# Two graph layers on one core: the second layer's preparation moved into the attention block, its roots on GpSimd, and fewer unused products at the start

## The chip, the core and the metric

The kernel runs on one core of a Trainium2 chip. TensorE (PE, with its weight loads PEld), VectorE (DVE), ScalarE (ACT) and GpSimd (POOL) each work through their own queue in order; SyncE (SP) issues the transfers. They meet at semaphores. The metric is the device time of one execution in microseconds, lower is better.

## What is computed

Two layers on x (4096 x 128 fp32) with one 0/1 adjacency matrix adj (4096 x 4096 int32). Layernorm has no scale or shift.

```python
h = relu(layernorm(x))
q, k, v = (h @ W.T + b for each)                       # 128 x 128 weights
scores = where(adj > 0, q @ k.T / sqrt(128), -9e15)
x = x + elu(softmax(scores, axis=-1) @ v)
h = relu(layernorm(x))
hw = h @ W
s1, s2 = hw @ a[:128], hw @ a[128:]
e = where(adj > 0, leaky_relu(s1[:, None] + s2[None, :], 0.01), -9e15)
x = x + hw + softmax(e, axis=1) @ h
```

## The kernel before, in words

x lies in SBUF as 32 tiles of 128 rows (T = 32), in 8 chunks of 4 tiles (NC = 8). A strip is one tile of query rows against all 4096 keys. The program has four blocks; at a block's end every engine waits for all.

**First stage** (`norm_and_project` with `x_in`, line 68). `constants_in` (line 390) starts with WARM = 36 products that nobody reads. Then, chunk by chunk: VectorE takes moments (`moments_of`), ScalarE the root (`roots`), VectorE the inverse, GpSimd normalises (line 104), TensorE transposes (`to_hT`, line 220) and makes the q, k and v products; ScalarE and VectorE copy out high and low parts. VectorE copies the turned weights (`copy_turned`, line 381) after its third chunk of moments, and TensorE's second transposes stand behind them. At the end come the extras: the turned weight of layer two, its product with a, and the bias row (`extras`, `copy_extras`). GpSimd makes the mask of strip 0 (`first_strip`).

**Attention block.** Each strip s has a period. TensorE (`period`, from line 863) makes strip s + 1's and s + 2's scores in four parts of 1024 columns (`make_scores`, 3 products per 512 columns, lines 810 to 812), turns strip s's weights (`turn`, `turn_high`, lines 821 and 837) and multiplies by v (`times_v`, lines 856, 857). VectorE adds the mask and finds the maximum (`add_mask`, line 726) and makes low parts (`low_part`, line 745, SBUF to SBUF; `turned_low`, line 738); ScalarE makes exponentials (line 647) and copies (lines 654, 661, 669). GpSimd's period is `add_elu(s - 2)`, `make_mask(s + 2)` (line 309), `add_halves(s - 1)` (lines 608, 610), `make_bytes(s + 3)` (line 304). SP loads adj, stores the mask bytes and turns the low parts by transposing transfers (`turn_low`). ScalarE's `elu_exp(s - 1)` closes its period, behind GpSimd's `add_halves(s - 1)`, and strip s + 1's first copies are queued behind it. The last strips have less to do: no mask for GpSimd after strip 29's period, no scores for TensorE after strip 30's.

**Second preparation** (`norm_and_project` again, without `x_in`). It begins when the attention block has ended. VectorE makes all 32 variances and the inverse roots, ScalarE the root, and then for each chunk: VectorE normalises (line 181), TensorE transposes, and the three jobs follow: `s_product` (s1 and s2 per row, 8 small products) with ScalarE's exponentials and VectorE's `weigh` (line 989, two instructions of 128 x 512); `s1_product` (s1 as a row on all partitions) with a copy and the signs; `hw_product` with VectorE's `hw_add` (line 1029). The signs compare each key's s2 with the queries' s1: for the first group of four strips `first_signs` and `first_sign` make 32 tiles of 128 x 512 bytes (ScalarE line 922 three of four, VectorE line 927 one). GpSimd's `split_words` (line 1018) makes the bf16 low parts of the weighed keys. SP loads the mask bytes of the first two groups by eight transposing transfers (`first_masks`). At the end `find_top` finds the largest s2 and a flag that chooses between the fast and a general path (always the fast one here), with three small products in between (`spread_top`), and cuts the first strip's mask.

**Second layer** (the `fast` functions). For each group g of 4 strips and strip b, VectorE's `cut(g, par, b)` combines mask bits and signs (`scale_mask`, `cut_lower`, `cut_upper`, lines 938, 942, 947), TensorE multiplies 64 pairs of tiles (line 1381), ScalarE copies the sums out (`copy_sums`, line 1316), VectorE forms the result and SP stores it. ScalarE's `body(g)` copies four strips' s1 (`s1_block`), and makes the signs of group g + 1, 11, 11 and 10 of them ahead of the sums of strips 0, 1 and 2. `cut(g + 1, ., 0)` waits for all 32 (`signs_ready`).

## Time and profile before

| | us |
|---|---|
| three runs | 771.25, 771.36 (median), 771.85 |
| the profiled execution | 769.68 |
| its span, first to last instruction | 767.9 |
| TensorE busy | 731.9 (95%) |
| VectorE, ScalarE, GpSimd busy | 564.3, 549.4, 432.9 |

"Busy" adds up an engine's instructions; a busy TensorE is one with a product under way, whatever its clock. The page cuts the span into 40 slices of 19.2 us and gives each engine's share in tenths, and beside it the TensorE clock that was granted. A timeline row has start, duration, engine, line, operation, output<-input and, in brackets, the engine's idle time before it and who released it. Where an engine's next instruction starts before the end of the one in front, rows overlap: the time from start to start is what the queue costs.

### The profile page before, as it was taken

To read this page: it belongs to the slowest core of one execution; us is meant where nothing else is said; L and a number is where in the kernel's file an instruction comes from. 1 tells how busy PE (TensorE), PEld (TensorE's weight loads), DVE (VectorE), ACT (ScalarE), POOL (GpSimd) and SP (SyncE) were. 2 spreads that over 40 slices of the span, in tenths; PEclk is the share of its full clock that TensorE was granted. 3 is DMA by queue.
4 is the path that set the end of the run, shared out by engine and by line. 5 is a ranking of instruction groups with operands and counts; after the bars stand their busy time and mean duration, and the time that the engine had idled before them with its cause. 6 is when DMAs were issued, how large, how long until landed. Compare 5 with 4: busy or idle time off the path is not lost. (4 is left out here: it accounts for less than half of the span.)

```text
span 767.9 us, 18394 instructions
## 1 busy us (share of the span) xinstructions
PE 731.9 (95%) x6301; PEld 616.8 (80%) x6301; DVE 564.3 (73%) x1199; ACT 549.4 (72%) x1063; POOL 432.9 (56%) x349
## 2 busy tenths in 40 slices
PE   8979999999999999999999997785999999999996
PEld 7658888888888888888888886554888888888885
DVE  5968787878878787877878784698477576577572
ACT  3846868787786878777786867685877977987910
POOL 5688799999999999999999963351000000000000
PEclk9989999999999999999999999697999999999999
DMA  6189998998979898887989742820253534433100
GB/s 234 60 286 252 243 269 240 280 252 253 258 251 262 235 279 238 276 257 245 258 252 269 220 97 56 168 53 0 63 91 65 94 76 80 92 74 80 38 10 13
DMA packets 189324, 130.88 MB, mean 170 GB/s; under 512 B 170336, under 2 KB 176992, under 8 KB 181088
## 3 DMA queue, kind: packets, MB, share of 16 engines
q1 hardware_dynamic: 188544, 130.05, 62.1%
q8 instruction: 25, 0.41, 0.2%
q10 hardware_dynamic: 576, 0.26, 0.1%
q14 instruction: 19, 0.16, 0.1%
q0 software_dynamic: 160, 0.00, 0.0%
HBM read 69.47 MB, written 18.87 MB: 115 GB/s over the span
## 5 line engine op out<-in xcount | busy, mean ns | idle before, releaser
L1381 PE MATMUL ps_x<-v,big 128*128 128x258 bf16 x2048 | 232.2, 275 | 2.3 <-issue 2.3
L1381 PEld LDWEIGHTS ps_x<-v,big 128*128 128x128 fp8e4 x2048 | 199.0, 98 | 32.6 <-issue 2.4
L726 DVE CUSTOM_DVE_ANT_0 scores<-ps_s,mask_neg 128x1024 f32<-128x1024 f32 x128 | 155.8, 1217 | 17.3 <-POOL mask_neg L309 17.0
L647 ACT ACTIVATE scores<-scores,neg_max 128x1024 f32<-128x1024 f32 x128 | 146.1, 1143 | 17.8 <-DVE neg_max L732 17.8
L745 DVE TENSOR_TENSOR low<-scores 128x1024 bf16<-128x1024 f32 x96 | 136.8, 1425 | 28.6 <-ACT scores L647 28.6
L309 POOL TENSOR_SCALAR mask_neg<-mask_bytes 128x2048 bf16<-128x2048 uint8 x64 | 153.3, 2396 | 5.4 <-POOL mask_bytes L304 0.4
L304 POOL TENSOR_SCALAR mask_bytes<-adj_sb 128x2048 uint8<-128x2048 int32 x64 | 148.2, 2332 | 3.4 <-POOLq L80 1.7
L661 ACT ACTIVATE hiT<-ps_t 128x512 bf16<-128x512 bf16 (+1 forms) x128 | 103.0, 805 | 53.4 <-PE ps_t L837 50.7
L856 PE MATMUL ps_acc<-v_parts,hiT 128*128 128x256 bf16 x768 | 140.4, 273 | 0.7 <-DMA lowT<-low 0.4
L922 ACT ACTIVATE big<-s_block,s_col 128x512 fp8e4<-128x512 f32 x224 | 139.4, 717 | 0.0
L857 PE MATMUL ps_acc<-v_parts,lowT 128*128 128x128 bf16 x768 | 133.6, 219 | 0.0
L810 PE MATMUL ps_s<-k_hi,q_strip 128*128 128x512 f32 x256 | 112.6, 440 | 3.6 <-DVE row_max L726 2.5
L812 PE MATMUL ps_s<-k_hi,q_strip 128*128 128x512 f32 x256 | 102.3, 400 | 0.0
L811 PE MATMUL ps_s<-k_lo,q_strip 128*128 128x512 f32 x256 | 101.0, 394 | 0.0
L856 PEld LDWEIGHTS ps_acc<-v_parts,hiT 128*128 128x128 bf16 x768 | 75.1, 98 | 8.6 <-issue 0.8
L857 PEld LDWEIGHTS ps_acc<-v_parts,lowT 128*128 128x128 bf16 x768 | 75.1, 98 | 0.7
L1316 ACT ACTIVATE sums<-ps_x,ac 128x258 f32<-128x258 f32 x64 | 26.6, 467 | 64.5 <-PE ps_x L1381 64.5
L738 DVE TENSOR_TENSOR pT_low<-ps_t,pT_high 128x512 bf16<-128x512 f32 x64 | 44.0, 687 | 31.1 <-ACT pT_high L654 31.1
L837 PEld LDWEIGHTS ps_t<-ident_half,scores 128*128 128x128 bf16 x768 | 44.9, 98 | 25.5 <-issue 25.1
L837 PE MATMUL ps_t<-ident_half,scores 128*128 128x128 bf16 x768 | 64.9, 221 | 0.0
L654 ACT ACTIVATE pT_high<-ps_t 128x512 bf16<-128x512 f32 x64 | 37.6, 590 | 34.8 <-PE ps_t L821 33.9
L810 PEld LDWEIGHTS ps_s<-k_hi,q_strip 128*128 128x128 f32 x256 | 48.9, 191 | 11.9 <-DVE row_max L726 3.3
(144 smaller groups left out, 1010.3 us busy)
## 6 DMA issues: line engine op xcount, KB each, us to landing
adj_sb<-in_adj SPq DMA_DIRECT2D x64, 1024.0 KB, 5.3
mask_bytes_dram<-mask_bytes SPq DMA_DIRECT2D x32, 512.0 KB, 2.9
x_sb<-in_x SPq DMA_DIRECT2D x8, 256.0 KB, 7.8
out<-res SPq DMA_DIRECT2D x32, 64.0 KB, 1.6
lowT<-low SPq DMA_TRANSPOSE x96, 4.7
big<-mask_bytes_dram SPq DMA_TRANSPOSE x32, 4.6
raw_w<-in_L_gnn_Wq ACTq DMA_DIRECT2D x1, 64.0 KB, 3.2
raw_w<-in_L_gnn_Wk ACTq DMA_DIRECT2D x1, 64.0 KB, 3.8
```

The costliest lines, as they stand in the source:

```text
L304: return nc.gpsimd.tensor_scalar(mask_bytes[par][:, half(h)], adj_sb[h][:], 1.0, 0.0, ALU.min, ALU.max)
L309: return nc.gpsimd.tensor_scalar(out, src, -NEG, NEG, ALU.mult, ALU.add)
L647: nc.scalar.activation(sc, sc, ACT.Exp, bias=neg_max[:, bn:bn + 1], accum_out=row_sum[:, bn, k:k + 1]).then_inc(exp_done, 1)
L661: nc.scalar.activation(hiT[k][:, half_of], ps_t[(2 + u) % 3][:].bitcast(BF16)[:, half_of], ACT.Copy).then_inc(hiT_ready, 1)
L726: nc.vector.tensor_tensor_reduce(out=scores[bn % 2][:, part(k)], in0=ps_s[k % 2][:], in1=mask[bn % 2][:, part(k)], scale=1.0, scalar=LOWES ...
L745: nc.vector.tensor_tensor(low[k][:], p, high_half(p), ALU.subtract).then_inc(low_done, 1)
L810: nc.tensor.matmul(o, high, k_hi[:, col], start=True, stop=False)
L837: last = nc.tensor.transpose(out[:, D * t:D * t + D], high[:, D * t:D * t + D], ident_half[:])
L856: nc.tensor.matmul(ps_a[:], high, v_parts[:, t, :, :], start=(i == 0 and n == 0), stop=False)
L857: last = nc.tensor.matmul(ps_a[:, 0, :], rest, v_parts[:, t, 0, :], start=False, stop=(i == NC - 1 and n == 3))
L922: return nc.scalar.activation(by_key_tile(lower[par], t), src.rearrange("p (s i) -> p s i", s=4), ACT.Sign, bias=s_col[:, t, 1:2], saturat ...
L1381: last = nc.tensor.matmul(ps_x[b % 2][k][:], by_key_tile(m, t)[:, b], v1[k][:, t, :].bitcast(BF16), start=(t == 0), stop=(t == T - 1))
```

## The change

The separate second preparation is taken away; its steps stand in the attention block's queues, around and behind the periods of the last strips.

- SBUF is laid out anew so that the preparation's tensors lie over tensors of the attention that are dead by then: h_sb over adj_sb, hT2 over scores[0], s1_row over the masks, v1 over q, the mask and sign tiles over k, scores[1] and v_parts. Four PSUM banks (`spare`) serve the first stage, the attention and the hw products in turn.
- Inverse roots are found without ScalarE's table, by a first guess from the bits (VectorE, `MAGIC`) and three Newton steps: for tiles 0 to 23 on GpSimd in the period of strip 29 (8 + 12 small operations on 24 columns, with VectorE's guess between them), for tiles 24 to 31 on VectorE at the end. GpSimd normalises chunks 0 to 2 in that period and 3 to 5 in the next; VectorE chunks 6 and 7. Both ScalarE table changes to Sqrt and back go.
- TensorE turns chunks 0, 1 and 2 and makes the first s products and the first 512 columns of s1 inside strip 31's period; ScalarE copies these out there.
- The last strip's attention output is finished by VectorE instead of ScalarE and GpSimd.
- Of s1 only the first 512 columns are made as a row by a product. The rest is stored from the column form to DRAM, one 4-byte element at a time (`store_s1`), and loaded back to all partitions in the second layer's block; ScalarE waits for it before group 1's and group 2's signs.
- Group 0's signs are made for strips 0 and 1 in the preparation, all 32 tiles by ScalarE, half as wide; those for strips 2 and 3 at the start of the second layer's block, 16 tiles on VectorE and 16 on ScalarE. In group 0 ScalarE makes group 1's signs 16 ahead of the sums of strip 1 and 16 ahead of those of strip 2, instead of 11, 11 and 10. Four of the eight hw additions move there too.
- Chunks 3 to 6 have one of two weighings on ScalarE.
- In the first stage WARM is 14, and the extras run inside chunks 3 to 5. At the start of the attention VectorE's `add_mask(1, 1, 1)` stands in front of `low_part(0, 0, 0)`.

```diff
-WARM = 36
+WARM = 14
...
+                def extras(pe, c):
+                    if c == 3:
+                        pe.wait_ge(weight_in, 16)
+                        nc.tensor.transpose(pw[:, 3 * D:4 * D], raw[3][:], ident[:]).then_inc(turn_done, 1)
+                    if c == 4:
+                        pe.wait_ge(turn_read, 4)
+                        pe.wait_ge(vectors_in, 16 * len(vectors))
+                        nc.tensor.matmul(pw[:, 0:2], turned[3][:], a_cols[:], start=True, stop=True)
+                        nc.tensor.matmul(pw[:, D:2 * D], ones[0:1, :], bv_row[:], start=True, stop=True).then_inc(extras_done, 1)
...
+                    def store_s1(cs, i):
+                        sp.wait_ge(s_out, cs.stop)
+                        for c in range(cs.start, cs.stop):
+                            sp.dma_start(s1_dram[c].rearrange("t p -> p t"), s_col[:, 4 * c:4 * c + 4, 0],
+                                         allow_slow_non_contiguous=True).then_inc(s1_stored[i], 16)
...
+                    sp.wait_ge(s_ready, 4 * T)
+                    for b in range(4):
+                        load_mask(sp, 0, b, 0)
+                    store_s1(S1_CHUNKS[0], 0)
+                    sp.wait_ge(t_done, TURNS * T)
+                    sp.wait_ge(low_done, 3 * T)
+                    for b in range(4):
+                        load_mask(sp, 1, b, 1)
+                    store_s1(S1_CHUNKS[1], 1)
...
+                    def inverse_root(cs):
+                        steps = Steps(pool, pool_tail)
+                        bn, moments, rstd = stats["bn"][:, cs], stats["moments"][:, cs], stats["rstd"][:, cs]
+                        mean_e, mean_o, m2_e, m2_o = (bn[:, :, i] for i in (1, 4, 2, 5))
+                        mean, var, apart, work = moments[:, :, 0], moments[:, :, 1], stats["root"][:, cs], newton[:, cs]
+                        pool.wait_ge(bn_done, cs.stop)
+                        steps.mark(nc.gpsimd.tensor_tensor(apart, mean_e, mean_o, ALU.subtract))
+                        steps.mark(nc.gpsimd.tensor_tensor(mean, mean_e, mean_o, ALU.add))
+                        steps.do(nc.gpsimd.tensor_tensor(var, m2_e, m2_o, ALU.add))
+                        steps.mark(nc.gpsimd.tensor_tensor(work, apart, apart, ALU.mult))
+                        steps.mark(nc.gpsimd.tensor_scalar(minus_mean[:, cs], mean, -0.5, 0.0, ALU.mult, ALU.add))
+                        steps.do(nc.gpsimd.tensor_scalar(var, var, 1.0 / D, EPS, ALU.mult, ALU.add))
+                        steps.do(nc.gpsimd.tensor_scalar(work, work, 0.25, 0.0, ALU.mult, ALU.add))
+                        steps.mark(nc.gpsimd.tensor_tensor(var, var, work, ALU.add))
+                        steps.wait()
+                        pool.sem_inc(var_made, 1)
+                        pool.wait_ge(seed_made, 1)
+                        for _ in range(3):
+                            steps.do(nc.gpsimd.tensor_tensor(work, rstd, rstd, ALU.mult))
+                            steps.do(nc.gpsimd.tensor_tensor(work, work, var, ALU.mult))
+                            steps.do(nc.gpsimd.tensor_scalar(work, work, -0.5, 1.5, ALU.mult, ALU.add))
+                            steps.do(nc.gpsimd.tensor_tensor(rstd, rstd, work, ALU.mult))
...
+                        if last_ones and s == T - 3:
+                            inverse_root(FIRST)
+                            pool.wait_ge(bytes_ready, 2 * T)
+                            for n in range(3):
+                                normalise(n)
+                        if last_ones and s == T - 2:
+                            for n in range(3, 6):
+                                normalise(n)
...
+                        if not ahead:
+                            act.wait_ge(low_done, 3 * T - 3)
+                            hT_out(0)
...
                             elu_exp(s - 1)
+                    def hT_out(c):
+                        act.wait_ge(x_turned, c + 1)
+                        nc.scalar.activation(hT2[:, 512 * c:512 * c + 512], turned_x[c % 2], ACT.Relu,
+                                             accum_out=hT_sum[:, c:c + 1]).then_inc(hT_ready, 1)
...
+                    def early_signs(c):
+                        act.wait_ge(s_out, c + 1)
+                        act.wait_ge(s1_out, 1)
+                        for t in range(4 * c, 4 * c + 4):
+                            last = sign_bytes(0, s1_row, t, EARLY)
+                        if c == NC - 1:
+                            last.then_inc(signs_ready, 1)
+                    def weigh(c):
+                        act.wait_ge(s_out, c + 1)
+                        for t in range(4 * c, 4 * c + 4):
+                            last = nc.scalar.activation(v1[0][:, t, 0:D], h_sb[:, t, :], ACT.Relu, scale=v1[0][:, t, D:D + 1])
+                        last.then_inc(weighed_by_scalar, 1)
                     all_periods(act, period)
-                    acc_copy(T - 1, 3)
-                    elu_exp(T - 1)
-                    use_table(1, ACT.Sqrt)
+                    s_out_of(0)
+                    act.wait_ge(s1_made, 1)
+                    nc.scalar.activation(s1_row[:, 0:512], ps_s3[1], ACT.Copy).then_inc(s1_out, 1)
+                    hT_out(2)
+                    act.wait_ge(last_att, 1)
+                    act.wait_ge(epi_done, T - 1)
+                    nc.scalar.activation(att_neg[:], att[:], ACT.Relu, scale=-1.0).then_inc(att_cut, 1)
+                    nc.scalar.activation(att_pos[:], att[:], ACT.Relu)
+                    act.wait_ge(att_cut, T)
+                    nc.scalar.activation(att_exp[:], att_neg[:], ACT.Exp, scale=-1.0).then_inc(last_parts, 1)
+                    s_out_of(1)
+                    hT_out(3)
+                    early_signs(0)
+                    for c in range(2, NC):
+                        s_out_of(c)
+                        if c + 2 < NC:
+                            hT_out(c + 2)
+                        if c in BY_SCALAR:
+                            weigh(c)
+                        early_signs(c - 1)
+                    early_signs(NC - 1)
...
+                    def last_attention():
+                        b = (T - 1) % 2
+                        inv = inv_by_parity[:, b:b + 1]
+                        dve.wait_ge(pv_done, 8 * T)
+                        dve.wait_ge(inv_ready, T)
+                        dve.wait_ge(halves_added, T - 1)
+                        dve.wait_ge(att_ready, T - 1)
+                        nc.vector.scalar_tensor_tensor(out=acc_sb[:, 0, :], in0=ps_a[:, 1, :], scalar=inv, in1=bv_rep[:],
+                                                       op0=ALU.mult, op1=ALU.add).then_inc(last_half, 1)
+                        dve.wait_ge(att_exp_ready, T - 1)
+                        dve.wait_ge(last_half, 1)
+                        nc.vector.scalar_tensor_tensor(out=att[:], in0=ps_a[:, 0, :], scalar=inv, in1=acc_sb[:, 0, :],
+                                                       op0=ALU.mult, op1=ALU.add).then_inc(last_att, 1)
...
                     add_mask(1, 1, 0)
+                    add_mask(1, 1, 1)
                     low_part(0, 0, 0)
-                    add_mask(1, 1, 1)
...
+                        if isinstance(c, int) and s == T - 3:
+                            dve.wait_ge(var_made, 1)
+                            first_guess(FIRST)
+                            tail.wait()
+                            nc.vector.sem_inc(seed_made, 1)
...
                     inverse_sum(T - 1, 3)
-                    for s in range(T - 3, T):
-                        dve.wait_ge(epi_done, s + 1)
-                        moments_of(s)
+                    dve.wait_ge(epi_done, T - 2)
+                    moments_of(T - 3)
+                    dve.wait_ge(epi_done, T - 1)
+                    moments_of(T - 2)
+                    aggregate(slice(LAST.start, T - 1))
+                    weigh(0)
+                    last_attention()
+                    weigh(1)
+                    last_elu()
+                    aggregate(slice(T - 1, T))
+                    add_eps(LAST)
+                    inverse_root(LAST)
+                    normalise(NC - 2)
+                    normalise(NC - 1)
+                    for c in range(2, NC - 1):
+                        weigh(c)
+                        if c >= 3:
+                            add_hw(c - 3)
+                    dve.wait_ge(s_out, NC)
+                    tail.mark(nc.vector.tensor_reduce(out=hT_total[:], in_=hT_sum[:], axis=AX.X, op=ALU.add))
+                    nc.vector.tensor_reduce(out=top[:, 0:1], in_=s_col[:, :, 1], axis=AX.X, op=ALU.max)
+                    tail.do(nc.vector.tensor_reduce(out=top[:, 1:2], in_=s_col[:, :, 0:2], axis=AX.XY, op=ALU.max,
+                                                    apply_absolute_value=True))
+                    nc.vector.tensor_scalar(hT_diag[:], ident[:], hT_total[:], None, ALU.mult).then_inc(top_ready, 1)
+                    weigh(NC - 1)
+                    dve.wait_ge(words_in[0], 64)
+                    scale_mask(0, 0).then_inc(scaled_ready, 1)
+                    dve.wait_ge(top_t, 1)
+                    nc.vector.tensor_copy(h_sum[:], ps_s2[:, D:2 * D])
+                    tail.do(nc.vector.tensor_reduce(out=top_turned[:], in_=ps_s2[0:2, 0:D], axis=AX.X, op=ALU.max))
+                    nc.vector.tensor_scalar(top_diag[:], ident[0:2, 0:2], top_turned[:], None, ALU.mult).then_inc(top_d, 1)
+                    dve.wait_ge(scaled_ready, 1)
+                    dve.wait_ge(signs_ready, 1)
+                    cut_lower(0, 0).then_inc(lower_ready, 1)
+                    dve.wait_ge(top_b, 1)
+                    tail.do(nc.vector.tensor_copy(top[:], ps_s2[:, 0:2]))
...
+                        if not ahead:
+                            pe.wait_ge(masked, 4 * T)
+                            turn_h(0)
...
+                        if not ahead:
+                            turn_h(1)
...
+                        if not ahead:
+                            s_products(0)
+                            nc.tensor.matmul(ps_s3[1], wa_rep[:], hT2[:, 0:512], start=True, stop=True).then_inc(s1_made, 1)
...
+                        if not ahead:
+                            turn_h(2)
...
+                    def turn_h(c):
+                        if c < NC - 2:
+                            pe.wait_ge(h_ready, c + 1)
+                        else:
+                            pe.wait_ge(h_by_vector, c - NC + 3)
...
+                        for i, cs in enumerate(S1_CHUNKS):
+                            sp.wait_ge(s1_stored[i], 16 * (cs.stop - cs.start))
+                            row = s1_dram[cs.start:cs.stop].rearrange("c t p -> (c t p)")
+                            sp.dma_start(s1_row[:, 512 * cs.start:512 * cs.stop], row.partition_broadcast(D)).then_inc(s1_in[i], 16)
...
+                        cut(0, 0, 1)
+                        for t in range(VECTOR_LATE):
+                            last = compare_bytes(nc.vector, 0, s1_row, t, LATE)
+                        last.then_inc(vector_late, 1)
+                        cut(0, 0, 2)
+                        add_last_hw(dve)
+                        cut(0, 0, 3)
...
+                        for t in range(VECTOR_LATE, T):
+                            last = sign_bytes(0, s1_row, t, LATE)
+                        last.then_inc(late_signs, 1)
...
+                                    first_group = isinstance(g, int) and g == 0
+                                    for t in (range(16 * b - 16, 16 * b) if first_group else range(11 * b, 11 * b + 11)):
+                                        if 0 <= t < T:
+                                            last = sign_bytes(1 - par, s1_block[:], t)
```

`first_guess` and `newton_step` are VectorE's two and three operations on 8 columns; `aggregate`, `add_eps`, `normalise` and `last_elu` are one instruction per tile or per step as their names say. `moments_of` increments `bn_done`.

## Rows read from the trace of the kernel before

**Rows 1.** The page, part 2: TensorE's granted clock in tenths, by slice of 19.2 us.

```profile
PEclk9989999999999999999999999697999999999999
```

**Rows 2.** Busy time by stretch: us, PE, PEld, DVE, ACT, POOL, PEclk, DMA share, GB/s.

```profile
96.00:150.00 54.00, 54.00 (x485) 45.80 (x484) 43.16 (x85) 41.60 (x84) 50.80 (x37) 1.00 0.89 258
...
528.30:534.00 5.70, 4.63 (x22) 3.29 (x23) 4.48 (x9) 3.76 (x8) 0.00 (x0) 0.50 0.00 0
...
540.00:761.60 221.60, 221.56 (x2001) 192.95 (x1998) 139.98 (x301) 157.70 (x286) 0.00 (x0) 1.00 0.32 67
```

**Rows 3.** The chain of waits (start us, us); the products' group (page, part 5).

```profile
529.37 59.88 PE ps_x L1381 x512
...
L1381 PE MATMUL ps_x<-v,big 128*128 128x258 bf16 x2048 | 232.2, 275 | 2.3 <-issue 2.3
```

**Rows 4.** Timeline of the first stage, TensorE, GpSimd and VectorE.

```profile
1.72 10.09 PE L393 MATMUL pw<-ident,ones 128*128 128x128 f32 x72 [1.72 <-POOL ones L339]
...
6.49 1.75 POOL L104 TENSOR_SCALAR xc<-x_sb,shift,rstd 128x128 f32<-128x128 f32 x4 [1.81 <-DVE shift L177]
...
12.62 0.29 DVE L381 TENSOR_SCALAR turned_w<-pw 128x128 f32<-128x128 f32 x1 [2.25 <-PE pw L398]
...
41.16 0.28 DVE L417 TENSOR_SCALAR wa_rep<-ident,wa 128x128 f32<-128x128 f32 x1
...
36.19 3.87 POOL L309 TENSOR_SCALAR mask_neg<-mask_bytes 128x2048 bf16<-128x2048 uint8 x2
```

**Rows 5.** Stretches by busy time, as Rows 2; timeline of TensorE.

```profile
1.70:5.40 3.70, 3.68 (x17) 3.68 (x18) 1.02 (x6) 0.53 (x2) 2.90 (x5) 1.00 0.86 274
...
43.00:46.20 3.20, 3.20 (x9) 2.52 (x8) 1.29 (x3) 0.00 (x0) 3.12 (x3) 0.51 0.75 246
...
41.75 0.47 PE L810 MATMUL ps_s<-k_hi,q_strip 128*128 128x512 f32 x1 [1.03 <-PEq L80]
```

**Rows 6.** Timeline of the first strips, TensorE.

```profile
57.20 0.79 PE L810 MATMUL ps_s<-k_hi,q_strip 128*128 128x512 f32 x1 [2.55 <-DVE row_max L726]
```

**Rows 7.** Timeline of the last strips, GpSimd and TensorE.

```profile
450.49 0.46 POOL L610 TENSOR_TENSOR att<-acc_sb,bv_rep 128x128 f32<-128x128 f32 x1
...
470.04 0.27 PE L856 MATMUL ps_acc<-v_parts,pT_high 128*128 128x256 bf16 x1 [1.86 <-ACT acc_sb L669]
...
477.37 0.22 PE L857 MATMUL ps_acc<-v_parts,lowT 128*128 128x128 bf16 x1
```

**Rows 8.** GpSimd's groups by form: busy us, mean ns of one, idle before.

```profile
L619 POOL TENSOR_TENSOR x_sb<-x_sb,att_exp 128x128 f32 x24 | 28.5, 1187 | 4.6 <-POOL att_exp L617 4.6
...
L104 POOL TENSOR_SCALAR xc<-x_sb,shift,rstd 128x128 f32<-128x128 f32 x32 | 13.9, 448 | 13.8 <-DVE shift L177 13.8
...
L334 POOL MEMSET eps<- 128x1 f32 x1 | 0.1, 98 | 0.3 <-POOLq L1428 0.3
```

**Rows 9.** Timeline of the preparation and its surroundings, ScalarE and VectorE.

```profile
469.42 0.47 ACT L669 ACTIVATE acc_sb<-ps_acc,inv_by_parity 128x256 f32<-128x256 f32 x1
...
491.43 1.95 ACT L922 ACTIVATE big<-s_row,s_col 128x512 fp8e4<-128x512 f32 x3
...
489.30 1.29 DVE L989 SCALAR_TENSOR_TENSOR v<-h_sb,v 128x512 f32<-128x512 f32 x2
...
527.62 0.15 DVE L1056 TENSOR_SCALAR flag<-top 128x1 int32<-128x1 f32 x1
```

**Rows 10.** SP's timeline; the transfers' sizes and landing; queue 1 (page, part 3).

```profile
482.08 19.98 SPq L933 DMA_TRANSPOSE big<-mask_bytes_dram  x8
...
adj_sb<-in_adj SPq DMA_DIRECT2D x64, 1024.0 KB, 5.3
...
q1 hardware_dynamic: 188544, 130.05, 62.1%
```

**Rows 11.** Timeline of the second layer's first group, ScalarE and VectorE.

```profile
539.94 6.84 ACT L922 ACTIVATE big<-s_block,s_col 128x512 fp8e4<-128x512 f32 x11
...
553.66 1.23 DVE L942 SCALAR_TENSOR_TENSOR big<-big 128x1024 uint32<-128x1024 uint32 x1 [3.54 <-ACT big L922]
```

514 lines of the change are left out of this document (271 added, 243 removed).

## The prediction

> **What bounds the kernel now.** I read the page's slices first [rows 1]. TensorE's clock is full in nearly every slice, with a dip about two thirds in, where it had stood idle. The stretches [rows 2] name it: in the attention TensorE is busy for the whole 54 us at full clock, GpSimd for 50.80; in the second layer's products, from 540, TensorE is busy for 221.56 of 221.60 us. Between them lies the second layer's preparation. The last attention product starts at 477.37 [rows 7], the first second-layer product at 529.37 [rows 3]. The chain of waits [rows 3] is TensorE's from there on: 232.2 us, which are 32 strips of 7.18 us and 2.4 us because the granted clock is 0.50 until 534 [rows 2]. So the end moves by as much as 529.37 moves, less any stall in the second layer. The profiled execution took 769.68 us with a span of 767.9; the runs' median is 771.36, 1.68 above it.
>
> **The start of the kernel.** The 36 unused products (72 passes) run from 1.72 to 11.65 at [rows 4]; 28 passes, 14 products, would be through at about 6.3, since 17 had started by 5.4 [rows 5] and the other 55 take the 6.3 us after it. The first transposes could go at 8.24, when GpSimd's first four tiles are made [rows 4]. The second transposes, at 13.4, waited for VectorE's copies of the turned weights, begun at 12.62; VectorE is free for them from 10.3. So the chain can start 2.3 us earlier. Against that, the remaining products leave TensorE idle for most of 6 to 11. At 38.4 to 41.75 a shorter gap, with 0.9 us of work in it, was followed by a granted clock of 0.51 from 43.0 to 46.2 [rows 5]. At that level the first chunk's 2.6 us of products take 5.2 and eat the gain; VectorE's round of 3.48 us a chunk bounds from the second chunk on. I take 0.2 us, bounds -1.0 (low clock for one chunk more) and +2.3 (no fall).
>
> The moved extras (weight of layer two, bias row, replicated column) ended the block: VectorE finishes at 41.44 and TensorE restarts at 41.75, while GpSimd's last mask ends at 40.06 [rows 4, 5]. Inside the chunks they cost VectorE some 1.2 us, of which 0.28 precedes what GpSimd waits for, and TensorE has slack of 0.4 us a chunk. The block then ends with GpSimd at 40.1, restart 40.4: **1.3 us** gained.
>
> The first strips: swapping the low part and the fifth mask addition lets the latter run at 52.3 instead of 55.93, where it stands behind a long low part; TensorE waited 2.55 us for it before 57.20 [rows 6]. VectorE's next step is then 1.0 earlier, TensorE up to 1.8: **1.4 us**. After that TensorE has no idle time, so both gains carry. Start in all: 0.2 + 1.3 + 1.4 = 2.9 us (bounds 0.5 and 5.5).
>
> **The tail of the attention.** Times below are on the old time axis, with the queues laid out in order. GpSimd is free at 450.98, its last mask made [rows 7]. It now does 20 small operations on 24 columns and 24 normalisations ahead of work that others need. The small operation has no row: a memset of one column takes 0.10, an addition of 128 columns 0.46 and comes every 0.53 with its wait [rows 7, 8]. I take 0.30 each, 24 columns being nearer the former in work but with a wait each. First eight: 2.4, to 453.4. VectorE, there at 451.8, waits 1.6, guesses (0.45) and goes on; its low part, at 452.38 before, and the mask addition behind it are 1.5 late, and 1.2 us of idle time before 456.25 takes up most of it. Twelve more: 3.6. Twelve normalisations at 0.435 [rows 8] are 5.2, times 1.4 since low parts run beside them: the same addition takes 0.46 alone and 1.19 beside VectorE's subtraction. That ends at 464.9; the exponential linear unit and the halves, 3.3 later, reach ScalarE at 468.2, where it needed them at 467.87: just in time. Twelve more end at 475.5, and strip 30's halves at 478.1, against 474.70 where ScalarE took them.
>
> The GpSimd engine's page in the Trainium skill, GPSIMD Engine Reference, section 3.1, gives 4497 ns for a two-input addition of 2048 fp32 columns. Taken off the 128-column row by that slope, 24 columns would be an estimated 0.23 us, 0.30 with the wait; the sum would be the same.
>
> TensorE gets three times four transposes (0.5 each at full clock), eight small products (0.85) and a 512-column one (1.0) in strip 31, 3.4 us, of which about 1 us falls into its idle 1.86 at 470.04 [rows 7]: the attention's last product ends at 479.7 instead of 477.4.
>
> **The path after it.** ScalarE's exponentials of strip 30 at 478.8 release GpSimd's sum at 480.4; VectorE follows with a statistic, seven aggregations (0.7), the first weighing (1.3, [rows 9]) and the last attention (0.75) to 483.5; ScalarE with 0.75 + 0.25 + 0.65 to 485.1. **From here ScalarE is the bound**: early signs of 32 tiles, each two strips wide; per chunk of four tiles that is 4 x p. The row has 0.61 for 512 columns (start to start, three in 1.95 with the last's tail) [rows 9], and a copy of 256 columns 0.47, of 512 0.60; I take p = 0.40, bounds 0.31 and 0.61. Up to the last score output: six chunks of signs 9.6, outputs 1.5, four hT outputs 2.6, four weighings on ScalarE 3.4, one wait 0.3: **502.6**. Then VectorE: tops 0.95, last weighing 1.3, scale 0.66, sums 0.7, cut 1.2, flag 0.34, cut 1.2 = 6.4: 509.0, plus 0.8 for GpSimd's queue, which has no slack left at 468.2: 509.8. The flag's last operation starts at 527.62 and TensorE starts at 529.37 [rows 3, 9], 1.6 us after it ends: first product at **511.4**, 18.0 earlier.
>
> VectorE's work from 485.8 to 502.6 (last strip's statistic and root 3.9, eight normalisations 2.3, weighings 4.1, additions 2.4: 12.7 us) fits beside it, and so does TensorE's, half of it at the low clock. SP's eight mask loads of 2.5 us [rows 10] end at 501.4 and are hidden; its last four element-wise stores follow 502.6. At nothing each they are hidden; at the mask loads' 2.5 they end 3 us behind VectorE. I take them hidden, as a plain transfer has no transposing to set up.
>
> **A stall that the change makes.** Half of group 0's signs are now made beside strips 0 and 1 (16 on each engine, 6.4 us on ScalarE: hidden), and group 1's signs start behind strip 0's sums. In the profile they start 0.95 after strip 0's product ends [rows 11]. Then 16 x 0.61 + 0.73 + 16 x 0.61 + 2.5 (the two cuts, 553.66 to 556.14) = 23.75 us after strip 0; strip 4 is due after 3 x 7.18 = 21.54. **TensorE waits 2.2 us**; before, it had 4 us to spare. The late VectorE work (16 comparisons, four additions) ends 17 us in, against 24 needed.
>
> **Sum.** 767.9 - 2.9 - 18.0 + 2.2 = 749.2; + 1.78 around the span = 751.0; + 1.68 to the median: **752.7 us**.
>
> **Rivals.** (a) Half-wide signs cost full price, p = 0.61: ScalarE's chain grows by 5.0 to the last output and by 0.9 behind it, the stall by 1: 760. For it: the output is byte-strided, so writing might bound. Against: copies shrink with width. 15%. (b) GpSimd's operations are dear (0.53 each, low parts doubling the normalisations): ScalarE stands behind strip 29's halves, TensorE's last product moves to 488, the block's end to 520.7: 764; half of that is likelier: 759. 15%. (c) The warm-up pays in full: 750.5. 8%. (d) SP's element-wise stores of s1 end the block: from 1.8 us each they do; at 4 us, 761. 7%. (e) **Slower than before**: the s1 row comes late. ScalarE may not start group 1's signs before the reloaded row (0.8 MB to 128 partitions) has landed. I expect 5 to 8 us after the block's start, behind a median landing of 5.3 for 1 MB [rows 10], and it is due after 9.6. Each us beyond stalls TensorE at strip 4 by one; from 20 us on the kernel is slower, 773 and up. For it: 1536 four-byte pieces must be written first. Against: they are issued 20 us before, and 188544 packets took 62% of 16 engines' span, 0.04 us each: 4 us [rows 10]. 2%. (f) The overlap doesn't come about, because each moved step waits for strip 31: about 770, 1%.
>
> On those stores the Trainium skill, DMA: Bandwidth & Descriptors, section Latency and other measured facts, says that a non-contiguous last dimension becomes one descriptor per element, which speaks against them; no row shows such a store.
>
> **Chances.** Forecast 52%, its own range 749 to 757. Range 747 to 763: it takes in (a), (b) at its likelier size, (c) and (d), and leaves out some 13%. A measurement tells 0.2% (1.5 us) apart. Faster 0.97, same 0.01, slower 0.02.
>
> **What would show it.** In the profile after: the first ps_x product near 508.5 (511.4 less 2.9) and an idle 2.2 us before strip 4's first product, released by VectorE's cut behind signs; half-wide signs started every 0.40; the last attention product near 477; TensorE's first attention product near 40.4 and none waiting 2.5 us after it; low clock about 9 to 15. If VectorE waits over 3 us for the variances, or ScalarE for the halves of strip 29, (b) holds. The prediction is wrong if another engine than ScalarE sets the pace from 485 to 502.

## The result, and the profile after

The changed kernel takes 764.38 us, the median of five runs (758.33 to 765.6), against 771.36 before (770.93 to 771.85). The ratio is 0.989, with a 95% interval of 0.985 to 0.993: faster by 7.0 us where 18.7 were forecast. Its executions lie 7 us apart, those of the kernel before under 1 us in that measurement. Timed twice more, beside the experiments, the changed kernel gave 765.3 (761.3 to 768.0) and 762.6 (758.7 to 763.7), and the kernel before 770.2 and 771.5, then with executions from 768.9 to 774.1. So both spread; the changed one spreads more.

Two profiles of the same changed kernel are read here. The first is its fastest execution: 758.33 us, span 756.5. The second, from the run called again5 below, took 763.7, span 761.9, near the median. The rows below have one line for each step of the forecast's sum, in order of time, from the timelines of TensorE, GpSimd and VectorE (start, duration, engine, line, operation, operands, and in brackets the idle time before it and what ended it). Fastest execution:

```profile
10.65 0.66 PE L185 MATMUL first_pt<-ident,scores 128*128 128x128 f32 x4 [1.75 <-DVE turned_w L422]
38.35 0.47 PE L1106 MATMUL ps_s<-k_hi,q_strip 128*128 128x512 f32 x1 [1.94 <-PEq L81]
57.65 0.28 PE L1152 MATMUL spare<-v_parts,pT_high 128*128 128x256 bf16 x1 [2.71 <-DVE pT_low L910]
60.55 0.27 PE L1152 MATMUL spare<-v_parts,hiT 128*128 128x256 bf16 x1 [0.38 <-DMA lowT<-low]
80.87 0.46 POOL L689 TENSOR_TENSOR att_exp<-att_exp,ones 128x128 f32<-128x128 f32 x1 [5.91 <-ACT att_exp L800]
441.18 0.47 POOL L689 TENSOR_TENSOR att_exp<-att_exp,ones 128x128 f32<-128x128 f32 x1 [0.32 <-ACT att_exp L800]
451.76 0.18 DVE L954 TENSOR_SCALAR seed<-moments 128x24 int32<-128x24 int32 x1 [1.28 <-POOLq L721]
481.82 0.35 DVE L991 SCALAR_TENSOR_TENSOR att<-spare,inv_by_parity,acc_sb 128x128 f32<-128x128 f32 x1
502.77 0.16 DVE L1075 TENSOR_REDUCE hT_total<-hT_sum 128x1 f32<-128x8 f32 x1 [1.53 <-ACT s_col L850]
507.50 0.29 DVE L1084 COPY h_sum<-ps_s 128x128 f32<-128x128 f32 x1 [1.19 <-PE ps_s L1244]
512.25 30.86 PE L1584 MATMUL ps_x<-q_parts,over_k 128*128 128x258 bf16 x256 [3.57 <-issue]
548.01 5.04 PE L1584 MATMUL ps_x<-q_parts,scores 128*128 128x258 bf16 x32 [4.91 <-DVE scores L328]
```

The same places in the execution near the median:

```profile
12.36 0.66 PE L185 MATMUL first_pt<-ident,scores 128*128 128x128 f32 x4 [2.43 <-DVE turned_w L422]
41.75 0.47 PE L1106 MATMUL ps_s<-k_hi,q_strip 128*128 128x512 f32 x1 [1.94 <-PEq L81]
64.85 0.37 PE L1152 MATMUL spare<-v_parts,hiT 128*128 128x256 bf16 x1 [3.98 <-DMA lowT<-low]
85.25 0.46 POOL L689 TENSOR_TENSOR att_exp<-att_exp,ones 128x128 f32<-128x128 f32 x1 [4.60 <-ACT att_exp L800]
446.12 0.46 POOL L689 TENSOR_TENSOR att_exp<-att_exp,ones 128x128 f32<-128x128 f32 x1 [0.30 <-ACT att_exp L800]
486.76 0.35 DVE L991 SCALAR_TENSOR_TENSOR att<-spare,inv_by_parity,acc_sb 128x128 f32<-128x128 f32 x1
507.72 0.16 DVE L1075 TENSOR_REDUCE hT_total<-hT_sum 128x1 f32<-128x8 f32 x1 [1.54 <-ACT s_col L850]
512.59 0.29 DVE L1084 COPY h_sum<-ps_s 128x128 f32<-128x128 f32 x1 [1.34 <-PE ps_s L1244]
517.33 31.01 PE L1584 MATMUL ps_x<-q_parts,over_k 128*128 128x258 bf16 x256 [3.58 <-issue]
553.26 2.92 PE L1584 MATMUL ps_x<-q_parts,scores 128*128 128x258 bf16 x13 [4.92 <-DVE scores L328]
```

The row POOL L689 is GpSimd's first step in the exponential linear unit of a strip: strip 0's at 80.87, strip 27's at 441.18. (The expectations below call the former that of strip 4; it is strip 0's.) In the kernel before they stand at 82.85 and 442.49. The reader is to see that the overlap came about: the first ps_x product (the second layer's products) is at 512.25 and 517.33, against 529.37 in [rows 3]. But in the second execution the attention is 3.6 us *later* than before (446.12 against 442.49), though it was forecast 2.9 earlier; and before strip 4 TensorE waits 4.9 us in both, where 2.2 were forecast. The wait of 2.71 at 57.65 follows two low parts on VectorE that took 2.51 and 2.31 us in a row, beside GpSimd's mask; near the median the same two took 1.22 each, and that wait is 1.61. No run was made to find out why.

Where TensorE's clock was low is read in windows; the columns are the window, the busy time of TensorE, its weight loads, VectorE, ScalarE and GpSimd with their counts, the granted clock, the DMA share and GB/s. Fastest execution, then the one near the median:

```profile
9.00:18.00 9.00, 7.35 (x38) 5.06 (x39) 7.37 (x34) 6.19 (x14) 4.78 (x12) 1.00 0.76 290
58.00:72.00 14.00, 13.62 (x124) 11.43 (x123) 12.28 (x21) 8.85 (x17) 11.64 (x7) 1.00 1.04 258
484.00:512.00 28.00, 23.11 (x114) 22.72 (x113) 20.71 (x51) 20.94 (x74) 16.35 (x14) 0.56 0.65 86
```

```profile
9.00:18.00 9.00, 6.18 (x24) 3.94 (x25) 5.32 (x28) 3.59 (x8) 4.44 (x11) 0.81 0.80 300
58.00:72.00 14.00, 9.67 (x73) 7.83 (x74) 7.62 (x16) 6.44 (x13) 11.44 (x6) 0.88 1.05 242
484.00:512.00 28.00, 26.48 (x138) 25.95 (x138) 20.96 (x56) 22.75 (x82) 17.51 (x16) 0.57 0.76 108
```

A granted clock of 0.81 over 9 us is 3.4 us at the low level (0.50, 1.2 GHz), 0.88 over 14 the same. The fastest execution had neither; it had 3.4 us of low clock between the two windows, from 38.7.

SP's queue, ScalarE's wait for the s1 row, and VectorE's last instruction of the block with its first of the next, in the fastest execution:

```profile
487.85 1.49 SPq L633 DMA_DIRECT2D s_row_dram<-s_col  x3
489.44 17.97 SPq L315 DMA_TRANSPOSE scores<-mask_bytes_dram  x4
507.45 2.23 SPq L633 DMA_DIRECT2D s_row_dram<-s_col  x4
512.09 8.06 SPq L1326 DMA_DIRECT2D mask_both<-s_row_dram  x2
523.53 0.63 ACT L1525 ACTIVATE s_block<-mask_both 128x512 f32<-128x512 f32 x1 [3.32 <-DMA mask_both<-s_row_dram]
509.66 1.23 DVE L328 TENSOR_TENSOR over_k<-over_k 128x1024 uint32<-128x1024 uint32 x1
512.59 0.24 DVE L1367 TENSOR_SCALAR z_top<-s_col,top 128x32 f32<-128x32 f32 x1 [1.71 <-issue]
```

Four transposing mask loads take SP 18 us, where eight took 20 before [rows 10]; and the s1 row, asked for at 512.09, is there at 523.5. ScalarE then starts on strip 0's sums at 524.3, though strip 0 was through at about 521.7. SP has issued its last store at 509.68, VectorE's last instruction ends at 510.89: VectorE ends the block, not SP.

### The profile page after: what moved, and what is told of

Its sections match the earlier page's. It is cut to its first block and busy times, and to the rows that moved or that the text cites. A ratio compares the mean times of both kernels' runs of the same rounds, so it can differ in the third digit from the quotient of the medians.

```text
span 756.5 us, 18346 instructions
## 1 busy us (share of the span) xinstructions
PE 724.9 (96%) x6243; PEld 616.0 (81%) x6243; DVE 558.8 (74%) x1190; ACT 549.0 (73%) x1090; POOL 448.9 (59%) x388
## 5 line engine op out<-in xcount | busy, mean ns | idle before, releaser
L898 DVE CUSTOM_DVE_ANT_0 scores<-ps_s,mask_both 128x1024 f32<-128x1024 f32 x128 | 155.8, 1217 | 17.4 <-POOL mask_both L350 17.4
L350 POOL TENSOR_SCALAR mask_both<-mask_bytes 128x2048 bf16<-128x2048 uint8 x64 | 153.3, 2396 | 5.4 <-POOL mask_bytes L345 0.4
L345 POOL TENSOR_SCALAR mask_bytes<-adj_both 128x2048 uint8<-128x2048 int32 x64 | 148.3, 2336 | 2.9 <-DMA adj_both<-in_adj 2.0
L1152 PE MATMUL spare<-v_parts,hiT 128*128 128x256 bf16 x768 | 140.3, 273 | 1.6 <-DMA lowT<-low 1.6
L784 ACT ACTIVATE hiT<-spare 128x512 bf16<-128x512 bf16 (+1 forms) x128 | 103.0, 805 | 50.9 <-PE spare L1133 48.3
L1153 PE MATMUL spare<-v_parts,lowT 128*128 128x128 bf16 x768 | 133.5, 219 | 0.0
L1584 PE MATMUL ps_x<-q_parts,over_k 128*128 128x258 bf16 x1024 | 117.4, 276 | 3.6 <-issue 3.6
L1584 PEld LDWEIGHTS ps_x<-q_parts,over_k 128*128 128x128 fp8e4 x1024 | 99.8, 98 | 19.2 <-issue 3.7
L304 ACT ACTIVATE v_parts<-s_block,s_col 128x512 fp8e4<-128x512 f32 x128 | 79.6, 717 | 0.0
L1153 PEld LDWEIGHTS spare<-v_parts,lowT 128*128 128x128 bf16 x768 | 75.2, 98 | 0.7
## 6 DMA issues: line engine op xcount, KB each, us to landing
mask_both<-s_row_dram SPq DMA_DIRECT2D x1, 768.0 KB, 11.4
```

Source lines behind the costliest of these rows:

```text
L304: return nc.scalar.activation(by_key_tile(lower[par], t)[:, strips], strips_of(src, strips), ACT.Sign, bias=s_col[:, t, 1:2], saturate=False)
L345: return nc.gpsimd.tensor_scalar(mask_bytes[par][:, half(h)], adj_sb[h], 1.0, 0.0, ALU.min, ALU.max)
L350: return nc.gpsimd.tensor_scalar(out, src, -NEG, NEG, ALU.mult, ALU.add)
L784: nc.scalar.activation(hiT[k][:, half_of], ps_t[(2 + u) % 3][:].bitcast(BF16)[:, half_of], ACT.Copy).then_inc(hiT_ready, 1)
L898: nc.vector.tensor_tensor_reduce(out=scores[bn % 2][:, part(k)], in0=ps_s[k % 2][:], in1=mask[bn % 2][:, part(k)], scale=1.0, scalar=LOWES ...
L1152: nc.tensor.matmul(ps_a[:], high, v_parts[:, t, :, :], start=(i == 0 and n == 0), stop=False)
```

## The experiments

All are edits of the changed kernel, but for one of the kernel before. Their times stand beside the kernel before on the same chip; each group of ratios is given with its 95% interval.

**A second and third profile.** again and again5 are the changed kernel unedited.

> The changed kernel itself, once more, for the profile of another execution. Its executions so far took 758.33 us (the profiled one, mean granted clock 0.975) and 763.5 to 765.6 (clock 0.966 to 0.971), while the kernel before stays within 1 us. Theory C (clock): the long executions spend some 6 to 14 us more at the low level. A long one's profile then shows one stretch more with the granted clock at 0.50 and TensorE busy in it, and no wait that is new: 6 us of it at the doubled price of each product make the 6 us. Theory D (transfer): the row of the second layer's first scores lands later in some executions than 11.4 us after its issue; a long one's profile then shows TensorE idle 9 to 12 us before strip 4 instead of 4.9.

> The changed kernel itself, beside the three below on the same chip. Expected 762 to 766 us, single executions from 758 to 768. Theory C (clock) of the first run, as it now stands: the first stage at the high level or not (first attention product at 38.4 or at 40.2 and later), the wait for the first transposing transfers (GpSimd's sum of strip 4 from 80.9 to 86.6), and 3.4 or 6.8 us of low level around strip 31 make the spread. The profile shows which of the three occurred, and their sum explains its span to within 1.5 us.

again: 765.3 us, ratio 0.992 (0.989 to 0.995). The profiled execution was the slowest of all, 767.98. It has the low clock for 3.4 us between 11 and 15, for 6.8 us from 62.7, for 6.8 us from 475.8, and the waits that all have before strip 4 (4.91) plus 1.50 before strip 3. again5: 762.6, ratio 0.988 (0.986 to 0.991). So theory C holds in part: the long executions have more low clock. But they have a longer transfer wait too: before the product that needs the first low part turned, TensorE waits 0.38 us in the fastest, 3.98 and 4.14 us in the others, and the clock falls behind it. Transfers and clock go together. Yet most of what lies between the fastest execution and again5's (5.4 us of span) is older: 3.4 us are there before the attention's first product (38.35 against 41.75), 1.0 more by GpSimd's sum of strip 0, and the rest of the way adds 1.0. Theory D falls: the wait before strip 4 is 4.91 or 4.92 in all three profiles.

**Warm-up.** warm36 sets WARM = 36 again; before_warm14 is the kernel before with WARM = 14; warm_even has

```
WARM = 20
...
last.then_inc(turn_done, 1)
for _ in range(6):
    nc.tensor.matmul(spare[0][:, 0:D], ident[:], ones[:], start=True, stop=True)
pe.wait_ge(turn_read, 3)
```

> The changed kernel with the 36 unused products of the first stage back, all else as changed. Theory A (the cut pays and costs nothing): the second chunk's transposes, at 10.65 in the changed kernel, go back to about 13.3, attention's first product from 38.35 to 40.5 to 41; the time is 1.3 to 2.5 us above the changed kernel's in executions of the same kind. Theory B (the cut costs clock): the spread of the changed kernel's executions over 7 us comes from the first stage; with 36 products all executions lie within 1.5 us of each other, and their median is below the changed kernel's 764.4, near 761.

> Edit of the kernel before, not of the changed one: 14 unused products instead of 36, nothing else. Theory C1: the clock falls in the first stage in most executions and takes back what the earlier second transposes give: they come at 10.6 to 12, attention's first product at 40.5 to 42 against 41.75, and the time is within 1.5 us of the kernel before, with executions 2 to 3 us further apart. Rival (the cut pays in full): first product at 39.4, the time 2.3 us below the kernel before.

> Edit: 20 unused products instead of 14 at the start, and six of 128 columns where TensorE waits for VectorE's copies of the turned weights. In six of eight profiles of kernels with 14 products the clock is low for 3.4 to 6.8 us somewhere between 10 and 17 us, and the attention's first product comes at 40.2 to 42.0; in the one without (the changed kernel's first profile) at 38.35; with 36 products the clock holds, but the second chunk's transposes are at 13.1 and the first product at 40.76. Theory C1 (the gap after the unused products costs the clock, the clock costs 2 us): here the clock stays at the high level until 36, the second chunk's transposes are at 10.6 to 11.1 and the attention's first product at 38.3 to 38.8. Rival C2 (what differs is when x and the weights arrive): the low clock goes, the first product stays at 40 to 42. In the time I expect under 1 us of either, since transfers bound the first strips (GpSimd's sum of strip 4 at 82 to 86 again).

warm36: 764.5, ratio 0.993 (0.991 to 0.995); second transposes at 13.09, first attention product at 40.76, no low clock in the first stage, executions 3 us apart. Its time is the changed kernel's, so neither A's 1.3 to 2.5 us nor B's gain shows. before_warm14: 769.5, ratio 0.998 (0.996 to 1.000), executions from 767.1 to 772.4. Its profile held the clock, had the first product at 39.56 instead of 41.75 and kept 1.77 of the 2.19 us to GpSimd's sum of strip 27. The cut alone is worth about 2 us in the kernel before, nearer to the rival's 2.3 than to C1's at most 1.5, and at the edge of what can be told. warm_even: 759.5, ratio 0.984 (0.980 to 0.988), clock full in the first stage, first product at 38.71, as C1 said; the time fell by more than the 1 us I expected, but its own executions lie 5.6 us apart, its profile was the slowest of them, and no unedited changed kernel ran on that chip, so that figure is loose. Over all profiles of this study: with 14 unused products eight of 14 have low clock between 10 and 17 (first attention product 40.2 to 42.0) and six don't (38.3 to 39.6); with 20 + 6 none of four has. In one of these (best, below) the product still came at 40.35, since a weight had landed late and the second transposes waited until 12.68. So C2 has a share beside C1.

**The first strips.** swap_back exchanges two lines on VectorE; turn_first moves one transfer on SP:

```
-                    add_mask(1, 1, 1)
                     low_part(0, 0, 0)
+                    add_mask(1, 1, 1)
```

```
 for h in range(2): load(0, 2, h)
 store(0, 1)
 turn_low(0, 0, 0)
 for h in range(2): load(0, 3, h)
```

> Edit: ahead of the attention's periods VectorE makes the first low part before the sixth mask addition again, as in the kernel before; all else as changed. In the profiles seen so far the changed kernel starts the attention 1.0 to 3.4 us earlier than the kernel before (38.35 to 40.8 against 41.75), and yet GpSimd's sum of strip 4, at 82.85 before, comes at 80.87, 83.5, 83.6, 85.3 and 86.6. Theory S (the swap costs): the low part, and with it the first transposing transfer, is late because of the swap; undone, TensorE's 3.3 to 4.4 us of waiting for lowT near 63 us go, and GpSimd's sum comes at 81 or 82 in each execution: 2 to 4 us in the time. Theory T (transfers bound the first strips): that wait stays at 3 to 4 us, since the transposing transfers stand behind the adjacency's on the queue and in the engines; TensorE's wait of 2.6 us for the mask addition comes back ahead of it and takes its place in part: the time is within 1 us of the changed kernel's.

> Edit: on SP's queue the first transposing transfer (strip 0's first low part) stands ahead of the two loads of strip 3's adjacency instead of behind them. In the slower profiles it is issued at 54.5 to 54.9, though the low part is done at 52.2. Theory T (transfers bound the first strips): it is issued at 52.3 and lands 2 us earlier, TensorE's wait near 63 us shrinks from 3.3 to 4.4 to about 2 us, and with it goes the low clock behind it: 2 to 4 us in the time. Rival: what it gains the later loads give back, GpSimd waits for strip 3's adjacency and the masks come late: no change or 1 us slower.

> The kernel of swap_back once more (the changed kernel with VectorE's first low part ahead of the sixth mask addition), for another profile and a surer time. best and best_noswap took the same time within 1 us, and best's profile had 43.3 us from the attention's first product to GpSimd's sum of strip 4, so the order alone no longer explains 41.1 against 42 to 45. Theory T (transfers and clock): this profile shows 42 to 45 us too where a wait of over 3 us for lowT is followed by the low level, and the time is 762 to 764, as the changed kernel's. Theory S (the swap costs): 41.1 us again and 761 or less.

swap_back: 762.7, ratio 0.989 (0.987 to 0.992); again as swap_back5: 762.3, 0.989 (0.986 to 0.992). turn_first: 762.1, 0.988 (0.985 to 0.992). The first profile of swap_back had 41.2 us from the first attention product to GpSimd's sum of strip 0, as theory S wanted; the second had 43.3 and this row:

```profile
61.60 0.37 PE L1152 MATMUL spare<-v_parts,hiT 128*128 128x256 bf16 x1 [2.70 <-DMA lowT<-low]
```

Theory S falls: the order on VectorE neither costs nor gains. What the stretch goes with is the wait for lowT. In the eight profiles where it is 2.7 us or more, the clock is low for 3.4 or 6.8 us behind it and that stretch takes 42.9 to 45.5; where it is 1.3 us or less, 40.9 to 42.5, with one exception (43.3, in best). That is a comparison of executions, not of an edit. turn_first has no such wait. The transfer is early as planned, 53.90 in this row against 54.51 in again, and three of them no longer stand in a row behind the loads; but TensorE then waits 2.62 us for VectorE. The gain in time is within the spread. So the wait for lowT can be moved away, but another stands behind it, and what bounds these strips in the end stays open.

```profile
53.90 1.36 SPq L608 DMA_TRANSPOSE lowT<-low  x1
55.31 1.50 SPq L593 DMA_DIRECT2D adj_both<-in_adj  x2
57.62 5.93 SPq L608 DMA_TRANSPOSE lowT<-low  x2
```

**The late row.** row_pe has TensorE spread chunk 1 of s1 and ScalarE copy it, so that group 1 doesn't need the load (second diff); turned_store stores s1 in another form (first diff):

```
+pe.wait_ge(s_out, NC)
+nc.tensor.transpose(turned_x[1][0:T, 0:D], s_col[:, :, 0], ident[:]).then_inc(s1_spread, 1)
+nc.vector.tensor_copy(s1_turned[:], turned_x[1][0:T, 0:D]).then_inc(s1_copied, 1)
-for c in range(cs.start, cs.stop):
-    sp.dma_start(s1_dram[c].rearrange("t p -> p t"), s_col[:, 4 * c:4 * c + 4, 0], ...)
+sp.dma_start(s1_dram.rearrange("c t p -> (c t) p"), s1_turned[:]).then_inc(s1_stored[0], 16)
```

```
+nc.tensor.matmul(ps_s3[1], wa_rep[:], hT2[:, 512:1024], start=True, stop=True).then_inc(s1_made, 1)
+nc.scalar.activation(s1_row[:, 512:1024], ps_s3[1], ACT.Copy).then_inc(s1_out, 1)
-if isinstance(g, int) and g < 2:
-    act.wait_ge(s1_in[g], 16)
+if isinstance(g, int) and g == 1:
+    for rows in s1_in: act.wait_ge(rows, 16)
```

> Edit: the 512 values of s1 that group 1's signs read are spread over the partitions by one more product on TensorE and one more ScalarE copy in the attention block, as it is done for group 0; the load from memory starts at group 2, and ScalarE doesn't wait for it in group 0. Theory L (the late row costs 2.5 us): in the changed kernel ScalarE starts on strip 0's sums at 524.30 though strip 0 is through at about 521.7, because it waits for the row until 523.51. Here it copies them at 521.8, TensorE's wait before strip 4 falls from 4.9 to 2.3 us and the time by 2.5 us. Theory M (the signs themselves bound): the wait stays at 4 to 5 us, since the 2 x 16 signs at 0.61 us and the two cuts take 23.1 us from ScalarE's start, and the earlier start is given back at the next wait. If theory D of the run above holds (the transfer makes the spread), all executions lie within 1.5 us of each other here.

> Edit: the 32 x 128 values of s1 are turned by one TensorE product and stored as 32 pieces of 512 bytes, instead of as seven stores of 512 single values. In the changed kernel the transfers behind each group of element-wise stores do nothing for 6 to 8 us (packets stop at 491 and go on at 497; they stop at 511, and the row's load, issued at 512.09, moves in full only from 519). Theory E (the element-wise stores hold up what stands behind them): SP's four transposing loads of group 1 take 9 to 10 us instead of 18, SP no longer ends the block, and the row lands 5 to 7 us after the block's start instead of 11.4: ScalarE doesn't wait for it, TensorE's wait before strip 4 is 2.3 us and none comes before strip 3: 3 to 4 us in the time. Rival W (the load itself is slow, one row read by 128 partitions): it still takes 10 us or more, the wait before strip 4 stays at 4.9.

row_pe: 759.0, ratio 0.985 (0.981 to 0.990). turned_store: 760.0, 0.986 (0.982 to 0.989). row_pe lies 6.2 us below again on the same chip, where 2.5 were expected; from the first ps_x product to the end its profile takes 241.3 us, the changed kernel's three 244.3, 244.6 and 246.3. Its executions still lie 6.8 us apart, so the row doesn't make the spread. In turned_store's profile, SP's queue, ScalarE's copy and TensorE before strip 4, and the landing of the row's load (size, us from issue):

```profile
489.54 10.61 SPq L317 DMA_TRANSPOSE scores<-mask_bytes_dram  x4
520.73 0.91 SPq L1328 DMA_DIRECT2D mask_both<-s_row_dram  x2
528.75 0.61 ACT L1527 ACTIVATE s_block<-mask_both 128x512 f32<-128x512 f32 x1
553.62 3.75 PE L1586 MATMUL ps_x<-q_parts,scores 128*128 128x258 bf16 x32 [2.31 <-DVE scores L330]
mask_both<-s_row_dram SPq DMA_DIRECT2D x1, 768.0 KB, 4.9
```

The four loads take 10.6 us, not 18. The row landed 4.9 us after its issue, not 11.4, and ScalarE's copy doesn't wait for it. In row_pe, where the element-wise stores stay, a smaller row (512 KB) still took 12.2. TensorE's wait before strip 4 is 2.31, in row_pe as well, and none comes before strip 3. Theories L and E hold, M and W fall: the row was late because it stood behind the element-wise stores, and the load itself is quick. The profile of the changed kernel shows the hold directly. Its packets by stretch:

```profile
DMA packets 1837, 0.01 MB, mean 4 GB/s; under 512 B 1837, under 2 KB 1837, under 8 KB 1837
DMA packets 0, 0.00 MB, mean 0 GB/s; under 512 B 0, under 2 KB 0, under 8 KB 0
DMA packets 7, 0.04 MB, mean 22 GB/s; under 512 B 0, under 2 KB 0, under 8 KB 7
DMA packets 102, 0.58 MB, mean 288 GB/s; under 512 B 15, under 2 KB 15, under 8 KB 86
```

These are 509 to 511 (the stores' single values, some 4 bytes a packet), 511 to 513, 517 to 519 and 520 to 522 us. The stores of 2 KB each landed 12.0 us after their issue (median).

**The strip-4 stall itself.** vs is turned_store with 13 + 13 tiles of group 1's signs on ScalarE and six on VectorE:

```
-for t in (range(16 * b - 16, 16 * b) if first_group else ...
+for t in (range(13 * b - 13, 13 * b if b < 3 else 0) if first_group else ...
+    for t in range(26, T):
+        last = compare_bytes(nc.vector, 1, s1_block[:], t, slice(0, 4))
```

> Edit: the turned store of s1 as in turned_store, and six of the 32 tiles of group 1's signs made by VectorE as comparisons, 13 and 13 left to ScalarE instead of 16 and 16. The sum behind the stall says 2 x 16 x 0.61 + 0.73 + 2.5 + 0.95 = 23.75 us against 21.54 that strip 4 is due; with 13 and 13 it is 20.1. If that sum is right, TensorE's wait of 2.31 us before strip 4 goes to 0, the second layer runs 32 strips of 7.18 us without a gap, and the time is 2.3 us below turned_store's (against the kernel before: a ratio near 0.983). Rival: VectorE's six comparisons of 512 columns take more than the 4 us of idle time it has there and delay its results, so that a wait of 1 to 3 us stays.

vs: 753.4, ratio 0.977 (0.972 to 0.981). There is no wait of TensorE between its first ps_x product and the end. Its profile is a clean pair with the fastest execution of the changed kernel, since the clock was low at the same places (38.7 to 42.1, 482.5 to 506.5, 509.8 to 516.6), except that it doesn't fall where the stall is gone. From the first ps_x product to the end it takes 237.7 us instead of 244.3: of these 6.6 us the stall is 4.9, and 1.3 are 3.4 us at 0.50 behind it, from 547 on (strip 4's first 32 products take 5.04 us instead of 3.74). Against turned_store the time is 0.9% of the kernel before lower, 7 us, where 2.3 were expected. The profiles give the edit 2.2 of them (239.9 to 237.7 us for that stretch); ahead of it both kernels have the same program, so the rest comes from executions and chips (the two ran on different ones), not from the edit.

**The preparation's clock, and the end of the block.** w_last puts TensorE's W products of the last two chunks between and behind the two products on the maxima; fill adds unused 512-column products to keep TensorE busy.

```
     hw_product(NC - 3)
-    hw_product(NC - 2)
-    hw_product(NC - 1)
     ... (products on top, hT_diag)
+    hw_product(NC - 2)
     ... (product on top_diag)
+    hw_product(NC - 1)
```

```
+def fill(c, n):
+    for _ in range(n):
+        nc.tensor.matmul(spare[c % 4][:], ident_half[:], hiT[0][:, 0:512], start=True, stop=True)
```

> Edit: of TensorE's last three chunks of W products, 4.88 us in a row at the low clock, one stays ahead of the two products on the maxima, one goes between them and one behind them. Theory Q (TensorE's queue delays the end of the block): VectorE waits 1.19 us for the first of them in the changed kernel, its copy of h_sum starting at 507.50; here it starts at 506.3 to 506.4 with no wait, the first ps_x product comes 1.1 us earlier (511.1 instead of 512.25, on that profile's axis), and the time is 1.1 us shorter. Rival: the block then ends with TensorE's last W product or with a wait in VectorE for the second product, and nothing is gained (within 0.3 us).

> Edit: unused products of 512 bf16 columns on TensorE, six each before and after the fourth chunk's transposes and five ahead of the W products of the first five chunks. Theory C (the clock in the preparation costs time): in the changed kernel TensorE runs at the low level from 482.6 to 506.5 and 509.9 to 516.7 and is busy for nearly all of 490 to 507, so that ScalarE waits 0.3 + 0.5 us and VectorE 1.2 us for it. With more to do it stays at the high level; the score output of the last chunk comes 1.0 to 1.5 us earlier, the W products behind it take 2.5 instead of 4.9, the first ps_x product comes 2 to 3 us earlier relative to the last attention operation on VectorE (30.4 us in the changed kernel's profile: 481.82 to 512.25), and the time falls by 2 to 4 us. Rival: the clock falls all the same, the 25 extra products take 0.43 us each, and the time is 5 us or more above the changed kernel's.

w_last: 764.1, ratio 0.991 (0.988 to 0.993): no gain. VectorE's wait for TensorE is gone, as theory Q said, but the rival holds:

```profile
509.74 0.28 DVE L1084 COPY h_sum<-ps_s 128x128 f32<-128x128 f32 x1
511.82 2.23 SPq L633 DMA_DIRECT2D s_row_dram<-s_col  x4
515.88 0.24 DVE L1367 TENSOR_SCALAR z_top<-s_col,top 128x32 f32<-128x32 f32 x1 [2.02 <-issue]
```

VectorE had its flag at 512.1 and the end of its last cut at 513.86; SP issued its last store until 514.05, and the next block began at 515.88, 2.02 us after VectorE instead of 1.71. VectorE itself gained only 0.5 of the 1.1 us (28.5 us from the last attention operation to the end of that cut, against 29.1), since the cut took 1.70 us instead of 1.23. fill: 763.3, 0.990 (0.986 to 0.994). The clock stayed full from 480 to 511. The stretch from the last attention operation on VectorE to the last score output took 20.0 us instead of 20.9, and the end stood behind SP again. So TensorE's low clock costs at least 0.9 us there. Where the clock is full for part of the stretch without unused products (row_pe, turn_first), it is 19.65: 1.3 less.

**Together.** comb1 is turned_store, turn_first and w_last; comb2 adds swap_back and vs; best adds warm_even; best_noswap is best without swap_back; best_fill is that with fill.

> Edit: turned_store, turn_first and w_last together. If each gain is its own (row and stores 3.5 to 5 us, first transposing transfer 2 us, W products behind the maxima 1.1 us once SP no longer ends the block), the time is 6 to 8 us below the changed kernel's 764.4 to 765.3: 757 to 758. The stretch from the last attention operation on VectorE to the first ps_x product, 30.4 us in every profile so far (w_last 30.2, fill 30.1: there SP's queue ended the block), is 29.4 here. Rival: the gains overlap (VectorE's own chain ends the block), that stretch stays at 30.2 or more.

> Edit: comb1, with VectorE's first low part ahead of the sixth mask addition as in the kernel before (swap_back), and with the 13 + 13 + 6 signs of vs. Expected if all four mechanisms stand: no wait of TensorE before strips 3 and 4 (2.3 us less than comb1), GpSimd's sum of strip 4 at 81 to 82.5 in spite of a first product at 40 to 42 (1 us less than comb1): 753.5 to 755. If swapping back and the early transfer do the same thing twice, comb2 is only 2.3 us below comb1.

> Edit: all five together: turned store and early first transposing transfer, W products behind the maxima, VectorE's first low part ahead of the sixth mask addition, 13 + 13 + 6 signs, and 20 + 6 unused products in the first stage. comb2 took 752.7 (750.2 to 754.9) without the last. If the clock in the first stage makes a part of the spread, as theory C says, the slower executions go and the median is 750 to 751.5; if what varies is elsewhere (transfers of the first strips, strip 31), it stays at 752 to 753.

> Edit: as best, but with the changed kernel's order: VectorE's sixth mask addition ahead of the first low part. From the attention's first product to GpSimd's sum of strip 4 the profiles with that order show 42.0 to 45.4 us (ten of them), those with the low part first 41.05 to 41.2 (three, the kernel before among them). Theory S (the swap costs): here 42.2 or more against 41.1 in best, and the time 1.2 to 2.5 us above best. Rival: with the transposing transfer already ahead of the loads on SP's queue the order no longer matters: within 0.7 us of best.

> Edit: best_noswap with the unused products of fill in the preparation. In fill's profile they held the clock at the high level from 480 to 511, the stretch from the last attention operation on VectorE to the last score output took 20.1 us instead of 20.95 (19.65 in the profiles where the clock stayed high by itself), and the gain ended at SP's queue, which stood behind VectorE. Here SP's queue is through early. If TensorE's level is what bounds that stretch, the time is 0.5 to 1.5 us below best_noswap's 752.3 and the executions lie closer together (within 3 us). Rival: the products stand in the way of the transposes ScalarE waits for, or the clock falls once the preparation is through and the first strips pay for it: 752 to 753, no gain.

| kernel | us, median (range) | ratio to before, 95% |
|---|---|---|
| comb1 | 757.0 (754.5 to 759.8) | 0.982 (0.978 to 0.987) |
| comb2 | 752.7 (750.2 to 754.9) | 0.977 (0.972 to 0.982) |
| best | 753.3 (751.6 to 753.7) | 0.977 (0.975 to 0.979) |
| best_noswap | 752.3 (750.4 to 754.6) | 0.977 (0.974 to 0.979) |
| best_fill | 752.7 (750.1 to 756.2) | 0.976 (0.973 to 0.978) |

comb1 came out as expected in time, but its stretch from the last attention operation to the first ps_x product is 30.2, not 29.4. VectorE's own chain ends the block. turned_store and vs, which put one more copy into it, have 30.8. Against vs, whose clock was low at the same places, w_last's order is worth 0.5 us. comb2 lies 4.3 below comb1. best doesn't lie below comb2: even clock in the first stage doesn't lower the median. best_noswap equals best, and its stretch in the first strips is the shorter one (40.9 against 43.3), the opposite of theory S. best_fill gains nothing. The other experiments leave vs and turned_store as the parts that count: all five kernels with both are 18 to 19.5 us faster than the kernel before, and best and best_noswap 9 to 10 us faster than the changed one on the same chip.

## Why the prediction was wrong

The forecast's own run was a span of 749.2. Against it stand 756.5 (fastest) and 761.9 (near the median), 7.3 and 12.7 us more. By milestone:

| | forecast | fastest | near the median |
|---|---|---|---|
| first attention product | 40.4 | 38.35 | 41.75 |
| GpSimd's sum of strip 0 (82.85 before) | 79.95 | 80.87 | 85.25 |
| the same of strip 27 (442.49 before) | 439.6 | 441.18 | 446.12 |
| last attention operation ends | 480.6 | 482.17 | 487.11 |
| last score output | 499.7 | 502.7 | 507.7 |
| first ps_x product | 508.5 | 512.25 | 517.33 |
| wait before strip 4 | 2.2 | 4.91 | 4.92 |
| span | 749.2 | 756.5 | 761.9 |

**Warm-up, 0.2 (bounds -1.0 to +2.3): right in kind.** The unused products end at 6.48; the rows give 6.7, where the prediction wrote 6.3, which changes nothing. The forecast put the low clock at 9 to 15. Eight of 14 profiles have it between 10 and 17, and it then eats the gain, as worked out; the others are rival (c). That it is one or the other from execution to execution was not foreseen. With late weights it made the first product of the one near the median 1.35 us later than forecast, of the fastest 2.05 earlier.

**Extras, 1.3: nearly right.** In warm36, which undoes the warm-up alone, the first product is at 40.76 against 41.75: 1.0.

**First strips, 1.4, and "after that TensorE has no idle time, so both gains carry": wrong, and with the late row the largest step.** (The mask addition that was swapped is the sixth, not the fifth.) The 2.55 us wait of [rows 6] went, as said, and returned as another: 2.71 for VectorE in the fastest execution, 3.98 for the turned low part in the one near the median, where the forecast saw "no idle time". What is late next, in the second, is the transfer of strip 0's first low part, issued behind strip 3's adjacency while the DMA engines are full (share 1.05 from 58 to 72). From the first product to GpSimd's sum of strip 0 the kernel before took 41.1 and 39.6 were forecast (79.95 less 40.4); the changed one took 42.5, 43.5 and 45.0, and no profile of this study less than 40.9. best against best_noswap shows the swap worth nothing. The sum of the start was +2.4 at that milestone instead of -2.9: 5.3 of the 12.7 us, 1.35 of them ahead of the first product and 3.95 in these strips. In comb2 and best_noswap the sum of strip 0 is at 79.5 and 79.8, as forecast, but because their first product came at 38.4 and 38.8: a coincidence, not the swap. Another 1.2 us (0.7 in the fastest) are lost over the next 27 strips. About 0.02 us per strip of that is a slower pace, 13.34 against 13.32 us, in all profiles with the changed attention. Its cause stays open.

**The tail of the attention: right.** GpSimd's small operations took 0.30 start to start but for two of twenty (1.10 and 1.23 long), VectorE waited 1.28 for the variances (1.6 forecast), and from strip 27's sum to the last attention operation it is 40.6 us, start to start, where the clock held, which is what the forecast has. Rival (b) is out. The unforeseen part is the clock: in the profiles with 6.8 us at the low level between 471 and 484 this stretch takes 43.0 to 43.7, with 3.4 us 41.2 to 41.4.

**ScalarE's pace, p = 0.40: right; that it all "fits beside it, and so does TensorE's": wrong by 1.5.** The early signs start every 0.40 to 0.41. But TensorE, at the low level from 482.5, needs 4.2 us a chunk there, and ScalarE waits 0.31 and 0.53 for it; 19.1 forecast from attention's end to last output, 20.6 measured, 19.3 where the clock was full for longer. After it, VectorE waits 1.19 and 1.34 for TensorE, whose last 24 W products (4.9 to 5.0 us in a row) stand before the ones on the maxima: from the last output to the first ps_x product it came to 9.5 against 8.8. **SP's stores "hidden": right, by little.** In the three profiles of the changed kernel they end 1.0 to 1.2 us ahead of VectorE's last instruction. Rival (d) didn't come about; but with VectorE sooner (w_last, fill) SP ends the block, 0.2 us behind it.

**The stall, 2.2: right, with a wait on top.** Without the late row it is 2.31 (row_pe, turned_store, comb1) and with 13 + 13 signs it is 0, so the sum 23.75 against 21.54 stands. **Rival (e) was put at 2% and decided 2.7 us of waiting, and the low clock behind it:** the row landed 11.4 us after its issue, when 9.6 after the block's start was the limit and 5 to 8 were expected. The step that failed is "against: they are issued 20 us before". Four of the seven stores are issued only 4.6 to 2.4 us before the row's load (507.45 to 509.68 against 512.09), and the load waits behind them. Another 1.2 us, the rest of the 12.7, lie behind the stall, where the clock falls; it fell behind none of the three waits of 2.31, so they belong to the late row too: 3.9 in all.

The Trainium skill, DMA: Bandwidth & Descriptors, section Rules for kernel authors (not the section that the prediction named), says that a strided or non-contiguous last dimension becomes one descriptor per element. The traces agree: 1837 packets that make up 0.01 MB between 509 and 511, and 12.0 us to land for 2 KB. The prediction had no term for what such stores do to the transfers behind them.

The range ended at 763 and missed by 1.4. It had no case in which a gain at the start turns into a loss, and it took the quiet first runs of the kernel before as a measure of the changed one's. The cases it did have were each priced alone; what happened was several at a time (start, row, clock behind waits).

## What to carry to other kernels

When a wait is taken away where the DMA engines are full, look for the next instruction or transfer that will be late, and price it before counting the gain. A long stall of TensorE can cost more than its length: the one of 4.9 us cost 6.2 with the low clock behind it, the one of 2.3 that was left cost 2.2. Don't put element-wise stores ahead of transfers that something waits for: turning the data first and storing 512-byte pieces costs one product and one copy (0.3 us at the end of the block) and removed both holds.

## What was not expected of the hardware

- Transfers issued behind element-wise stores on SP's queue moved almost nothing for 6 to 8 us after most of the stores' packets had gone (in the fastest execution from 493 to 499 and from 511 to 519), twice in each profile that has them, transposing loads and plain ones alike. With the stores gone, the same four loads took 9.5 to 11.3 us instead of 17.1 to 19.1, and the row landed in 4.0 to 5.9 instead of 10.6 to 13.2. Why the queue holds them is open.
- TensorE's clock fell behind some waits and not others in executions of the same kernel: behind one of 2.70 us in the first strips of swap_back5, not behind one of 2.71 in the fastest execution; behind every wait of 4.57 to 4.92 before strip 4 (for 3.4 to 6.8 us), behind none of 2.31 there. The Trainium skill, TensorE: Matmul & The Clock Gate, Part 1, says that the number of products at the low clock at a kernel's start varies from run to run, and puts what that start costs under 1% of a typical span. Here the clock falls in the middle of the kernel too: the executions of one kernel, 758.3 to 768.0, are 1.3% apart, and the low clock is a part of that.
